# Feed-forward of a gated two-layer block: the order of integer and halved tiles at a step's start

## The reference

```python
def act_quant(x):
    scale = 127.0 / jnp.clip(jnp.max(jnp.abs(x), axis=-1, keepdims=True), 1e-05)
    return jnp.clip(jnp.round(x * scale), -128, 127) / scale
def weight_quant(w):
    scale = 1.0 / jnp.clip(jnp.mean(jnp.abs(w)), 1e-05)
    return jnp.clip(jnp.round(w * scale), -1, 1) / scale
...
h = bit_linear(x, w1)                                  # 512 -> 2048 channels
h = depthwise_conv1d(h.transpose(0, 2, 1), conv_w, conv_b)   # 3 taps along the tokens
h = jax.nn.silu(h.transpose(0, 2, 1))
return bit_linear(h, w2)                               # 2048 -> 512
```

## Time and profile before

| | us |
|---|---|
| runs | 1670.02, 1670.09, 1677.87 |
| median | 1670.09 |
| profiled execution, its own time | 1673.33 |
| its span | 1671.7 |
| PE busy in the span | 1510.4 (90%) |
| DVE busy | 1053.8 (63%) |
| ACT busy | 815.9 (49%) |
| POOL busy | 743.7 (44%) |
| mean granted clock of PE, of full | 0.935 |

### The profile page before, as it was taken

The page is one execution under the profiler, slowest core; times in us unless marked ns, Lnnn a source line. Parts: engine busy times, 40 slices in busy tenths (PEclk is TensorE's granted clock), DMA queues, the critical chain, the costliest instruction groups (busy, mean ns, idle before and its releaser), DMA issues. The chain is left out here.

```text
span 1671.7 us, 24835 instructions
## 1 busy us (share of the span) xinstructions
PE 1510.4 (90%) x8764; PEld 1147.7 (69%) x8764; DVE 1053.8 (63%) x1759; ACT 815.9 (49%) x1448; POOL 743.7 (44%) x666
## 2 busy tenths in 40 slices
PE   6589999999978999989999999988888789999997
PEld 5478788788756888867787788765554455555553
DVE  3468878788728564332332333247996899999995
ACT  2145555555522221213343444325777778888883
POOL 0044344435414675243414100255551878888870
PEclk9789999999978999999999999995766889999998
DMA  3157656666326999735535333459772111111112
GB/s 142 46 182 252 210 207 252 228 212 230 127 85 216 355 356 345 247 120 176 179 105 169 119 107 107 138 145 319 235 258 92 38 39 38 64 63 63 52 51 101
DMA packets 131428, 270.31 MB, mean 162 GB/s; under 512 B 16083, under 2 KB 31443, under 8 KB 129288
## 3 DMA queue, kind: packets, MB, share of 16 engines
q1 hardware_dynamic: 100168, 175.47, 31.2%
q0 software_dynamic: 16624, 62.93, 10.7%
q10 hardware_dynamic: 14544, 30.68, 4.9%
HBM read 145.56 MB, written 122.42 MB: 160 GB/s over the span
## 5 line engine op out<-in xcount | busy, mean ns | idle before, releaser
L243 PE MATMUL e_u_ps<-e_xs,w_shared 128*128 128x512 f32 x720 | 169.4, 396 | 6.4 <-DVE e_sg L1262 6.4
L243 PEld LDWEIGHTS e_u_ps<-e_xs,w_shared 128*128 128x128 f32 x720 | 137.6, 192 | 35.4 <-DVE e_sg L1262 6.5
L2357 PE MATMUL f_banks<-b_xdT,w1h 128*128 128x512 f32 x512 | 146.0, 427 | 14.5 <-POOL b_xdT L2107 9.7
L2133 POOL TENSOR_TENSOR b_h<-b_h,b_srow 128x512 f32<-128x512 f32 x112 | 143.3, 1333 | 26.3 <-ACT b_srow L2169 26.3
L1458 PE MATMUL e_u_ps<-e_w,e_xs 128*128 128x512 f32 x528 | 133.0, 401 | 2.0 <-DVE e_xs L1354 1.2
L2357 PEld LDWEIGHTS f_banks<-b_xdT,w1h 128*128 128x128 f32 x512 | 97.1, 196 | 48.2 <-POOL b_xdT L2107 14.1
L2326 PE MATMUL b_o_ps<-w2q,b_h 128*128 128x512 bf16 x448 | 116.9, 384 | 8.7 <-ACT b_h L2163 8.7
L2158 ACT ACTIVATE b_h<-b_h 128x512 f32<-128x512 f32 x128 | 88.2, 690 | 53.4 <-DVE b_h L2248 52.4
L1362 DVE TENSOR_TENSOR e_hT<-e_r_ps,e_hT 128x256 fp32r<-128x256 f32 x69 | 29.3, 424 | 134.5 <-ACT e_hT L1200 134.5
L1458 PEld LDWEIGHTS e_u_ps<-e_w,e_xs 128*128 128x128 f32 x528 | 95.7, 188 | 23.2 <-DVE e_xs L1354 1.6
L2245 DVE SCALAR_TENSOR_TENSOR b_h<-f_banks,cw,b_h 128x511 f32<-128x511 f32 x128 | 95.2, 744 | 22.1 <-ACT b_h L2152 22.1
(11 more groups left out here) (267 smaller groups left out, 3504.5 us busy)
## 6 DMA issues: line engine op xcount, KB each, us to landing
slots_in_scratch<-e_xs SPq DMA_DIRECT2D x22, 1024.0 KB, 8.3
e_xe<-slots_in_scratch SPq DMA_DIRECT2D x69, 256.0 KB, 2.7
experts_out_scratch<-e_ye ACTq DMA_DIRECT2D x69, 256.0 KB, 2.0
yx_a<-in_w POOLq DMA_DIRECT2D x10, 1024.0 KB, 5.9
xin<-in_x SPq DMA_DIRECT2D x16, 512.0 KB, 5.0
xres<-in_x SPq DMA_DIRECT2D x16, 512.0 KB, 5.3
x_scratch<-x SPq DMA_DIRECT2D x32, 256.0 KB, 3.4
xn_scratch<-xn SPq DMA_DIRECT2D x32, 256.0 KB, 2.0
```

The costliest lines, as they stand in the source:

```text
L243: mm = pe.matmul(n.u_ps[:, (2 * q + j) % 4], ws[q // n.KH][:, pa, at:at + P], xs[:, pb, k], start=(k == 0 and (pa, pb) == PASSES[0]), stop ...
L2133: pool.tensor_tensor(ht, ht, srow[:], ALU.mult).then_inc(u_done, 1)
L2357: mm = pe.matmul(f_ps[:, v % RING], n.w1h[:, k, (c - NV) * P:(c - NV + 1) * P], xdT[:, part, k], start=(k == 0 and part == 0), stop=(k == ...
```

## The change

The table that gives positions to channel tiles is another permutation. Eight tiles of sixteen stay integer ones.

```diff
-    MIXED = (0, 1, 8, 2, 9, 10, 3, 11, 4, 12, 5, 13, 6, 14, 15, 7)
+    MIXED = (0, 1, 2, 8, 9, 3, 10, 4, 11, 5, 12, 13, 6, 14, 15, 7)
```

## The result

| | before | changed |
|---|---|---|
| runs | 9 | 9 |
| median, us | 1673.36 | 1678.05 |
| lowest to highest, us | 1670.02 to 1677.87 | 1676.87 to 1683.33 |
| ratio, 95% interval | | 1.0032, 1.0017 to 1.0047 |
| profiled execution: span, us | 1671.7 | 1676.2 |

The changed kernel is slower by 0.32%, 4.7 us between the medians, clear of the noise and less than 0.5%. The forecast of the difference was 3.3 us. The forecast of the time, 1673.4, was worked out from a median of 1670.09 in three runs of the kernel before; the nine runs have 1673.36, so the measured 1678.05 lies 4.65 above it, and 3.27 of that is the starting value.

A forecast was written before the change was run, and what follows sets the result against it. No engine alone bounds it: a 42.94 us loop of waits runs over PE, DVE and ACT. Steady steps 6 x 0.50 = 3.0 us plus step 1's 0.3 give 3.3 over the 1670.09 median: 1673.4 us, range 1667 to 1680.

The forecast's parts named there:

- Place one: Start of a step, positions 2 and 3: PE's 1.2 us stall only moves, cost nothing; rival of stall gained 0.10.
- Place two: Ahead of the first part-maximum: position 9's token scale waits for PE, +0.50 us per loop, 3.0 us in all.
- the two waits on DVE: Steady step: 1.0 to 1.3 us at the scale before the first part-maximum, 0.3 to 0.5 before tile 6's taps.
- Step 1: Without down matmuls DVE sets the pace: one more token scale, +0.6 less 0.26 of standing, +0.3 us.
- Nothing swallows it: Place two's 0.50 us reaches the row of token scales and the loop; rival that it is swallowed, 1670, chance 0.14.
- no other: Sign in a steady step: ACT's wait for tile 8's taps grows by 0.5 us and no other wait of ACT grows.
- The clock: Rival: PE's clock falls at the transposes, 2.66 us in each of steps 2 to 6, 13.3 in all, 1686.7; chance 0.08.

The follow-up runs named there:

- place two alone: Kernel before with only positions 5 to 10 ordered as in the changed kernel, positions 2 and 3 kept; ratio 1.0017, loop 43.28 us.
- the maximum before the scale: Changed kernel with DVE's first part-maximum issued ahead of the token scale of position 9; ratio to before 0.9989, loop 42.11 us.
- the filled kernel: Changed kernel with seven more bf16 matmuls per steady step between PE's single down matmuls ahead of the transposes; ratio to before 1.0023, loops 43.32 to 43.36 us.

## Why the prediction was right, point by point

- **Place one costs nothing**: right. Alone it leaves the loop at 42.82. The stand moved to where it was said to, in front of ACT's lifts, and with ACT's queue loosened the loop went to 42.18, near the 42.1 expected: the queue was the hold.
- **Place two costs the difference of 1.94 on PE and 1.44 on DVE**: right, nearly to the row. PE's part measured 1.93; the part-maximum came 0.48 later against the transposes, 0.50 forecast; the two waits on DVE were 1.11 and 0.36, forecast 1.0 to 1.3 and 0.3 to 0.5. The loop took 0.44. So each of steps 2 to 7 was over-sized by some 0.06, and the 3.0 for them became 2.6. The loop of place two alone shows this cost by itself.
- **Step 1**: +0.24 measured, +0.3 forecast.
- **Nothing swallows it**: right. But ACT's wait for tile 8's taps grew from 2.15 to 3.00, by 0.85 and not by 0.5:

```profile
1445.30 0.70 ACT L2158 ACTIVATE b_h<-b_h 128x512 f32<-128x512 f32 x1 [3.00 <-DVE b_h L2248]
```

Counted from the transposes, ACT also reaches this wait 0.37 earlier, since neither the middle taps of 8 nor the taps of 7, which its silu of 7 needs, now stand behind a scale's wait. And two other waits of ACT for taps came ahead of it, 0.60 and 0.45 us (none and 0.20 before), where the prediction had said "no other".

- **The clock** is where the prediction was short, and one of its own signs of being wrong, a granted clock under 1.00 in the steady steps, was met. The low clock was a rival, all or nothing, at 0.08 with 2.66 us in each of five steps, and the sum had nothing for it. It came in between: in 1 or 2 of five steps, 1.6 us each, 1.5 x 1.6 = 2.4 us in the mean of four executions. With 2.9 of the other terms that is 5.3. The end of the program, from the first part-maximum of step 7 on, gave back 0.6 and 0.5 in two executions and took 0.2 and 0.1 more in the others. In all the feed-forward part was 5.0 longer in the mean, against the 4.7 of the medians. That the measured difference lies so near the forecast is in part luck: nothing in the prediction said that the clock would fall in only one or two of the five steps, and in all five, at 1.6 us each, it would have cost 8 us in place of 2.4.

The argument against this rival was that in the kernel before stands of 1.29 and 0.83 at the end of step 1 had left the clock full. That can't be put down to shorter stands around them: with 0.87 for POOL between them and 0.17 behind, they add up to 3.2 us in the 10 us ahead of the transposes, where those of the changed kernel ahead of the fall add up to 2.4. In the changed kernel itself the stands ahead of step 2's transposes are longer than those ahead of step 4's, and in none of its four executions did the clock fall there (second execution):

```profile
1374.28 1.04 PE L2351 MATMUL f_banks<-xqT,w1v 128*128 128x512 bf16 x4 [1.67 <-DVE b_h L2248]
...
1379.13 1.20 PE L2357 MATMUL f_banks<-b_xdT,w1h 128*128 128x512 f32 x4 [0.91 <-DVE b_h L2248]
...
1382.93 0.41 PE L2326 MATMUL b_o_ps<-w2q,b_h 128*128 128x512 bf16 x1 [0.82 <-ACT b_h L2163]
```

And in place two alone, with the clock full, the stands add up to 2.5 us, but those close ahead of the transposes are shorter, 0.38 and 0.17:

```profile
1457.31 1.04 PE L2351 MATMUL f_banks<-xqT,w1v 128*128 128x512 bf16 x4 [0.73 <-DVE b_h L2248]
...
1461.22 0.74 PE L2357 MATMUL f_banks<-b_xdT,w1h 128*128 128x512 f32 x2 [0.68 <-POOL b_xdT L2107]
1462.47 0.73 PE L2357 MATMUL f_banks<-b_xdT,w1h 128*128 128x512 f32 x2 [0.51 <-POOL b_xdT L2107]
...
1466.00 0.41 PE L2326 MATMUL b_o_ps<-w2q,b_h 128*128 128x512 bf16 x1 [0.38 <-ACT b_h L2163]
```

So neither the longest stand nor the sum tells where the clock falls. Place one moves stands next to the transposes, place two makes the one at position 1 longer, 0.73 in place of 0.26 us; neither alone showed a fall, nor did the kernel with the maximum before the scale, where the stand at position 1 is gone. That it takes both is what these rows suggest, but there is one execution of each of the three, and it is not shown.

What stays open is why steps 4 and 6 and never 2, 3 or 5, and which of the stands weighs how much.

## What to carry to other kernels

On an engine that works in order, ask of each instruction that waits for another engine what stands behind it and does not need it: here a 3.3 us reduction stood behind a scale's wait for PE, and changing the two made a loss of 0.4 us a step into a gain of 0.7. A visible stand is worth what the next wait on the same path leaves of it: a stall of 1.2 us was moved away whole for nothing, since the queue of another engine ended at the same time as before. Where a change gathers stands of PE in one place, look at the granted clock of every repetition, not of one.

## What the runs showed that was not expected

The clock fell in the same step of the changed kernel in four executions out of four, and in none of the same five steps of eight other kernels, the one before among them, in 10 executions (three of the filled kernel, one of each other).

The parts ahead of the feed-forward, the same code in all kernels, moved whole times by more than the change did: the first part-maximum of step 0, ahead of all that was edited, began at 1309.13 us in one profiled execution and at 1320.73 in another, and the kernel before ran from 1669.7 to 1679.46 us in 35 runs. The loop repeated to 0.05 us between executions with the same clock.
